# A four-layer recurrent network on one core: the first layer's tail is folded into its experts, and the last layer's attention gets another order on TensorE

## The chip, the core and the metric

The kernel runs as one program on one core of a Trainium2 chip. The metric is the device time of one execution in microseconds (us); less is better. The engines that compute are TensorE (PE in the profile; its weight loads stand apart as PEld), VectorE (DVE), ScalarE (ACT) and GpSimd (POOL); SyncE (SP) issues the transfers. Semaphores are all that orders the engines between each other.

## What is computed

The input is x of 8 sequences by 512 tokens by 128 features. Each of four layers normalises x, runs an attention `s` and a feed-forward part `f` on the same normalised xn, and adds their gated product:

```
xn = layernorm(x)
s = attention_l(xn, ...)
g = silu(ffn_l(xn, ...))
x = x + s * g
```

Two pieces matter here.

The first layer's attention (differential, 16 heads of 8) ends in a normalisation of each head's output and a projection; its feed-forward part has two shared experts of weight 1/2 and four routed ones, of which a token takes the two with the largest softmax weight:

```
normed = (heads - mu) * rsqrt(var + EPS) * ln_w + ln_b
attention = normed.reshape(b, s, H * DH) @ wo
weights = softmax(x @ gate_w + gate_b);  topk_w, topk_i = top_k(weights, 2)
shared = (relu(x @ sw1 + sb1) @ sw2 + sb2).sum(axis=2) / 2
routed = (gather(relu(x @ rw1 + rb1) @ rw2 + rb2, topk_i) * topk_w).sum(axis=2)
```

The last layer's attention is causal, with 16 heads of 64 and a relative bias:

```
logits = (einsum('bhqd,bhkd->bhqk', q, k) + causal + bias) / dh
out = einsum('bhqk,bhkd->bhqd', softmax(logits), v)
return out.reshape(B, T, H * dh) @ Wo + bo
```

## The kernel before, in words

A sequence's 512 tokens are four blocks of 128 (`QT = 4`). Each layer is a row of phases; a phase is a block of its own with its own tiles and semaphores, and no engine begins the next one until all have ended the last. `R.xnT` holds xn with the features on the partitions, `R.s` and `R.f` the two results. Within a phase each engine has a program written out by hand; `run_bodies` writes the first and the last trip apart and loops over those between. There is no scheduler: the order on an engine is the order of its code.

**First layer's tail.** After `attend_phase` has left the heads' outputs in `heads`, five phases follow. `outproj_phase` (L889, "out") goes through the 8 sequences: DVE centres (`center`, L917 and L919), ACT squares (L970), DVE sums (L925), ACT takes the root (L976), DVE inverts and scales (L929, L933), PE transposes four blocks (`turn`, L1020), ACT moves them out of PSUM (`leave`, L983), PE multiplies by `wo` (`project`, L1028), and ACT copies the result to `R.s` (L989). `logits_phase` (L1052, "lg") computes the gate, four values a token, with the gate's weights as the loaded operand and xn as the moving one, and turns them back (L1072, L1079). `top2_phase` (L1103, "top") takes the softmax and the two largest on DVE. `turn_weights_phase` (L1190, "turn") transposes the weights and multiplies them by the output biases, which gives the first content of `R.f` (L1255, L1263, L1224). `experts_phase` (L1269, "ex") runs the six experts in three trips of two. A trip has 16 groups `g` (two experts by eight sequences); a group has four steps `u`: `up` (L1331, 128x512) into one of two PSUM banks `ph`, ReLU on ACT (L1366), `down` (L1340, four of 128x128) into `po`; one `up` goes ahead of each `down`. DVE adds the weighted `po` into `R.f` once a group (L1382).

**Last layer's attention** (`layer3_attention`, L1872, "att"). For each of 8 sequences it runs 8 pairs of heads, 64 pairs `m` in all, and each pair has four steps `j`, one for each block of queries; `s` counts the steps of a sequence. Because of the causal mask step j is (j+1)*128 keys wide. For a pair PE does: three projections into the one bank `pA` (k=0 gives qT, k=1 kT, both L1985; k=2 gives v, L1988), each moved out by ACT (`leave`, L2089); for each step the `scores` (L2000), whose two heads take the upper and the lower 64 rows of the array, three steps ahead (`AHEAD`); `turn` of the two heads' softmax rows (L2010); `weigh` (L2027), whose two heads take 64 columns of the array each, into `pO`; and once a pair `through_wo` (L2036), which also goes to `pA`. ACT moves `pO` out (`outputs`, L2111). DVE adds the bias and finds the row's extreme (`extreme`, L2160), inverts the row sums (`invert`, L2166), adds `pA` to `R.s` (`add`, L2180) and copies the turned rows to `WT` (L2174; for step 1 it is ACT, L2105). ACT takes the exponentials (`expo`, L2097), POOL divides (L1958). `WT` is a ring of four rows, two a step. The order around a step is

```
if j % 2 == 1: scores(s + 3); scores(s + 4)
if j == 0: project(1, m + 1)
if j == 1: through_wo(m - 1)
if j == 2: project(2, m + 1)
if j == 3: project(0, m + 2)
turn(2 * s + 2); turn(2 * s + 3)
weigh(s)
```

## Time and profile before

| | |
|---|---|
| median of 3 runs | 3879.37 us (3876.12 to 3881.76) |
| the profiled execution's own time | 3873.31 us |
| its span | 3871.5 us |
| mean granted TensorE clock | 0.914 of 2.4 GHz |
| busy PE, DVE, ACT, POOL | 87%, 61%, 52%, 40% of the span |
| first layer's tail, from the last write to `heads` to the last write to `R.f` | 678.2 to 1104.7 us |
| last layer's attention, steady part | 3017 to 3786 us |

The profiled execution is one run with every instruction's start and duration in it. Its time is 1.8 us above its span and 6.1 us under the median. A share of busy time is a mean over stages that have different limits, so the stages are read apart.

### The profile page before, as it was taken

How to read it: one execution, taken by the hardware profiler on the slowest of the kernel's cores; microseconds unless marked ns; L12 is line 12 of the kernel's file. 1: busy time of each engine (PE TensorE's matmuls, PEld its weight loads, DVE VectorE, ACT ScalarE, POOL GpSimd, SP SyncE). 2: the span in 40 equal slices, each digit the busy share in tenths (PEclk: the TensorE clock that was granted, in tenths of full speed). 3: DMA queues.
4: the chain of work that ended last, by engine and by line, in shares of the span. 5: the costliest groups of instructions: out<-in, count | busy, mean ns of one | idle time of the engine just before them, and what ended most of it. 6: DMA issues, size and time to landing. Idle time of an engine off the chain costs nothing. (4 is left out here: it accounts for less than half of the span.)

```text
span 3871.5 us, 87522 instructions
## 1 busy us (share of the span) xinstructions
PE 3381.1 (87%) x26932; PEld 2090.2 (54%) x26932; DVE 2358.0 (61%) x5961; ACT 2030.5 (52%) x4194; POOL 1567.7 (40%) x2652
## 2 busy tenths in 40 slices
PE   5799999599966999959999947979874999999997
PEld 2344444477742222226777723579863666666664
DVE  5688887311135888856777765258356566666664
ACT  5588888333353788833333353333253566666552
POOL 0367676000010232316777717045472444444440
PEclk9799999799986999979999968877696999999999
DMA  5422222000013111116666411300023333333330
GB/s 138 102 73 74 73 73 54 12 6 12 6 36 89 45 44 46 41 27 173 163 156 161 117 58 37 102 12 3 9 50 55 127 115 114 118 115 113 114 101 22
DMA packets 199845, 289.31 MB, mean 75 GB/s; under 512 B 40954, under 2 KB 156864, under 8 KB 199252
## 3 DMA queue, kind: packets, MB, share of 16 engines
q1 hardware_dynamic: 195480, 277.41, 25.8%
q0 software_dynamic: 4096, 8.40, 1.5%
q8 instruction: 158, 2.59, 0.3%
q14 instruction: 111, 0.91, 0.1%
HBM read 234.41 MB, written 35.93 MB: 70 GB/s over the span
## 5 line engine op out<-in xcount | busy, mean ns | idle before, releaser
L779 ACT ACTIVATE att_E<-att_pX,att_gs 128x512 f32<-128x512 f32 x1152 | 718.7, 684 | 128.3 <-PE att_pX L708 127.6
L1958 POOL TENSOR_TENSOR att_E<-att_E,att_rz 128x128 f32<-128x128 f32 (+3 forms) x512 | 358.2, 721 | 433.6 <-DVE att_rz L2166 433.6
L834 DVE TENSOR_REDUCE att_mx<-att_pS 128x2 f32<-128x1024 f32 (+2 forms) x448 | 434.6, 991 | 82.2 <-PE att_pS L686 68.3
L686 PE MATMUL att_pS<-arr_ks,arr_qs 72*128 72x512 bf16 (+4 forms) x1536 | 421.4, 338 | 51.8 <-DVE att_mx L834 28.4
L708 PE MATMUL att_pX<-arr_qs,arr_ks 75*128 75x512 bf16 (+4 forms) x1536 | 419.2, 328 | 8.5 <-DMA arr_qs<-att_mp 4.4
L1698 POOL TENSOR_TENSOR pairs_h<-pairs_m,pairs_r 128x512 f32<-128x512 f32 x272 | 346.1, 1273 | 190.9 <-DVE pairs_m L1761 181.7
L1722 PEld LDWEIGHTS pairs_po<-pairs_a,pairs_h 128*128 128x128 f32 x2176 | 286.3, 192 | 130.3 <-issue 128.5
L826 DVE CUSTOM_DVE_ANT_0 att_seen<-att_pS,arr_later 128x384 bf16<-128x384 f32 (+1 forms) x512 | 298.8, 613 | 80.3 <-PE att_pS L686 79.9
L1743 ACT ACTIVATE pairs_r<-pairs_ph 128x512 f32<-128x512 f32 x272 | 162.6, 598 | 327.1 <-PE pairs_ph L1714 327.1
L721 PE MATMUL att_pO<-att_E,att_vs 128*9 128x512 f32 (+3 forms) x3072 | 296.8, 488 | 8.8 <-ACT att_E L779 8.4
L2097 ACT ACTIVATE att_E<-att_S,att_nm 128x128 f32<-128x128 f32 (+3 forms) x512 | 282.1, 556 | 39.6 <-DVE att_nm L2160 39.4
L1714 PE MATMUL pairs_ph<-xnT,pairs_a 128*128 128x512 f32 x544 | 281.4, 600 | 10.2 <-DMA pairs_a<-in_down_dram 10.2
L1722 PE MATMUL pairs_po<-pairs_a,pairs_h 128*128 128x128 f32 x2176 | 287.5, 275 | 0.3 <-POOL pairs_h L1698 0.3
L617 POOL TENSOR_SCALAR_AFFINE_SELECT att_E<-att_E 128x256 f32<-128x256 f32 (+1 forms) x640 | 228.5, 361 | 136.4 <-ACT att_E L779 131.1
L686 PEld LDWEIGHTS att_pS<-arr_ks,arr_qs 76*128 76x128 bf16 (+1 forms) x1536 | 133.9, 98 | 258.9 <-DVE att_mx L834 100.0
L1761 DVE SCALAR_TENSOR_TENSOR pairs_m<-pairs_ph,pairs_c 128x512 f32<-128x512 f32 x272 | 187.9, 692 | 140.4 <-ACT pairs_r L1743 132.2
L2160 DVE CUSTOM_DVE_ANT_0 att_S<-att_pS,att_bias 128x128 f32<-128x128 f32 (+3 forms) x512 | 230.5, 487 | 67.4 <-PE att_pS L2000 62.0
L708 PEld LDWEIGHTS att_pX<-arr_qs,arr_ks 127*128 127x128 bf16 (+1 forms) x1536 | 149.0, 98 | 217.0 <-ACT att_E L779 124.4
L1340 PEld LDWEIGHTS ex_po<-ex_a,ex_h 128*128 128x128 f32 x1536 | 201.6, 192 | 91.8 <-issue 91.0
L1366 ACT ACTIVATE ex_h<-ex_ph,ex_bs 128x512 f32<-128x512 f32 x192 | 132.0, 687 | 213.5 <-PE ex_ph L1331 213.5
L1382 DVE SCALAR_TENSOR_TENSOR f<-ex_po,ex_ws,f 128x128 f32<-128x128 f32 x192 | 54.1, 344 | 276.7 <-PE ex_po L1340 276.7
L2174 DVE COPY att_WT<-att_pT 128x128 f32<-128x128 f32 (+2 forms) x384 | 178.8, 507 | 66.2 <-PE att_pT L2010 59.0
(410 smaller groups left out, 6531.1 us busy)
## 6 DMA issues: line engine op xcount, KB each, us to landing
pairs_c<-weights SPq DMA_DIRECT2D x272, 256.0 KB, 4.0
att_bias<-in_bias_dram SPq DMA_DIRECT2D x64, 896.0 KB, 4.6
parts<-proj_part SPq DMA_DIRECT2D x144, 128.0 KB, 2.3
att_xb<-xnT SPq DMA_DIRECT2D x64, 256.0 KB, 2.7
arr_qs<-parts SPq DMA_DIRECT2D x192, 64.0 KB
arr_ks<-parts SPq DMA_DIRECT2D x192, 64.0 KB
att_w<-in_w3a_dram SPq DMA_DIRECT2D x64, 192.0 KB, 2.4
arr_qs<-parts SPq DMA_DIRECT2D x96, 96.0 KB
```

Source lines behind the costliest of these rows:

```text
L686: ins = nc.tensor.matmul(pS[:, bank, n * w:(n + 1) * w], qs[:K1, u, x, q * P:(q + 1) * P], ks[:K1, u, x, :w], start=(n == 0 or not causal) ...
L708: ins = nc.tensor.matmul(pX[:, bank, o:o + w], ks[:, g % NB, x, kt * P:(kt + 1) * P], qs[:, g % NB, x, q0(kt):], start=(n == 0), stop=True ...
L721: ins = nc.tensor.matmul(pO[32 * x:32 * x + DV, q0(kt):], vs[:, g % 2, x // maps, kt], E[:, cell_of[x, kt] % NE, o:o + w], start=(kt == OR ...
L779: nc.scalar.activation(E[:, c % NE], pX[:, BANK2[(g * NP2 + c) % (NB * NP2)]], ACT.Exp, scale=gs[:, g % 2, gain_of:gain_of + 1]).then_inc( ...
L826: V.tensor_tensor_reduce(out=seen[:, own, :w], in0=pS[:, bank, :w], in1=arr.later[:, T - w:], scale=1.0, scalar=-3.0e38, op0=ALU.add, op1= ...
L834: V.reduce_max(dst, src, AX.X).then_inc(s_mx, 1)
L1698: nc.gpsimd.tensor_tensor(h[:, g % RING], m[:, g % RING], r[:, g % RING], ALU.mult).then_inc(s_h, 1)
L1714: nc.tensor.matmul(ph[:, g % RING], a[:, v, 0], R.xnT[:, b * T:(b + 1) * T], start=True, stop=True).then_inc(s_up, 1)
L1722: ins = nc.tensor.matmul(po[:, g % RING, q * P:(q + 1) * P], h[:, g % RING, q * P:(q + 1) * P], a[:, v, 1], start=True, stop=True)
L1958: nc.gpsimd.tensor_tensor(E[:, k, :width(j)], E[:, k, :width(j)], rz[:, u, k:k + 1].broadcast_to([P, width(j)]), ALU.mult).then_inc(s_n, 1)
L2097: nc.scalar.activation(E[:, k, :width(j)], S[:, r % RING, :width(j)], ACT.Exp, bias=nm[:, u, k:k + 1], scale=-1.0, accum_out=Z[:, u, k:k + ...
L2160: nc.vector.tensor_tensor_reduce(out=S[:, r % RING, :w_], in0=pS[:, r // 2 % 2, h, :w_], in1=bias[:, u, off:off + w_], scale=-1.0 / DW, sc ...
```

## The change

In the first layer, `first_tail_phase` takes the place of all five phases. The experts' order is turned: the shared two come first (first trip), the routed four after them. Before the experts PE computes the gate by 32 small matmuls, with xn as the loaded operand and the four gate columns as the moving one; into the first trip's 16 groups are put the normalisation and projection of the 8 sequences, a piece after a step of a group, and the softmax and choice of the two largest. Their functions `center`, `variance`, `scale`, `square`, `root`, `leave`, `result` are those of `outproj_phase`; `top_two` and `shifted` are `top2_phase`'s. The output biases are now added by DVE, four 128x128 instructions a group in the second and third trip; the shared experts' bias `c2` comes in with the first write of `R.f`. `ph` and `h` have four buffers in place of two, and two `up`s go ahead.

In the last layer, `weigh` of two steps stands together at every even step, two steps late, with the next two `scores` right behind; all three projections of a pair move by a place, and `WT` has eight rows. `through_wo` now waits for the pair's v to have left `pA`.

```diff
-        outproj_phase(nc, R, "out0", heads, out)
+        first_tail_phase(nc, R, "ex0", heads, out, gate, t["lower4"], t["w1_0"], t["b1_0"], t["w2_0"], t["b2_0"])
...
+def first_tail_phase(nc, R, name, heads, out, gate, lower, w1, b1, w2, b2):
...
+    NE, NR, U, HB = 6, 4, 4, 4
...
+        ph = p.ps("ph", [P, HB, T])
         po = p.ps("po", [P, 2, T])
-        s_b = p.sem("b")
+        pT = p.ps("pT", [P, T])
+        pY = p.ps("pY", [P, QT, D])
...
+        pl = pY[:, :, :].rearrange("p q d -> p (q d)")[:, :NT * NR]
...
                 sp.dma_start(bb[:, :, :], b1).then_inc(s_b, 16)
+                sp.dma_start(lo[:, :], lower).then_inc(s_lo, 16)
...
+                    if first:
+                        sp.dma_start(b2r[:, :, :], b2).then_inc(s_b2, 16)
...
+                pe.wait_ge(s_g, 32)
+                for n in range(NT):
+                    ins = nc.tensor.matmul(pl[:, n * NR:(n + 1) * NR], R.xnT[:, n * P:(n + 1) * P], gw, start=True, stop=True)
+                ins.then_inc(s_lg, 1)
+                pe.wait_ge(s_o, loads)
+
+                def turn(n):
+                    pe.wait_ge(s_hb, n + 1)
+                    if n >= 1:
+                        pe.wait_ge(s_hT, n)
+                    for q in range(QT):
+                        ins = nc.tensor.transpose(pT[:, q * P:(q + 1) * P], hb[:, n % 4, q], R.ident[:, :])
+                    ins.then_inc(s_t, 1)
+
+                def project(n):
+                    if n == 0:
+                        pe.wait_ge(s_sub, 1)
+                    pe.wait_ge(s_hT, n + 1)
+                    if n >= 1:
+                        pe.wait_ge(s_out, n)
+                    for q in range(QT):
+                        ins = nc.tensor.matmul(pY[:, q], hT[:, n % 2, q * P:(q + 1) * P], wo, start=True, stop=True)
+                    ins.then_inc(s_y, 1)
...
-                        if not (first and k < 2):
-                            pe.wait_ge(s_h, at(IT * U, k - 1))
-                        nc.tensor.matmul(ph[:, u % 2], a1[:, v, u], R.xnT[:, b * T:(b + 1) * T], start=True, stop=True).then_inc(s_up, 1)
+                        if not (first and k < HB):
+                            pe.wait_ge(s_h, at(IT * U, k - HB + 1))
+                        nc.tensor.matmul(ph[:, u], a1[:, v, u], R.xnT[:, b * T:(b + 1) * T], start=True, stop=True).then_inc(s_up, 1)
...
                     if first:
                         up(0)
+                        up(1)
                     for k in range(IT * U):
-                        if not (last and k + 1 >= IT * U):
-                            up(k + 1)
-                        down(*divmod(k, U))
+                        g, u = divmod(k, U)
+                        if not (last and k + 2 >= IT * U):
+                            up(k + 2)
+                        down(g, u)
+                        if first and u == 1 and 0 <= g - 4 < B:
+                            turn(g - 4)
+                        if first and u == 3 and 0 <= g - 5 < B:
+                            project(g - 5)
...
+                            if not first:
+                                continue
+                            if g == 0 and u == 3:
+                                act.wait_ge(s_sub, 1)
+                                nc.scalar.activation(pr[:, :, :], pr[:, :, :], ACT.Exp).then_inc(s_exp, 1)
+                            if u == 0 and 0 <= g - 1 < B:
+                                square(g - 1)
+                            if u == 1 and 0 <= g - 6 < B:
+                                result(g - 6)
+                            if u == 2 and 0 <= g - 4 < B:
+                                leave(g - 4)
+                            if u == 3 and 0 <= g - 2 < B:
+                                root(g - 2)
...
+                        if first:
+                            if g == 0:
+                                V.memset(eps[:, :], EPS).then_inc(s_eps, 1)
+                                shifted()
+                                shared_bias()
+                            if g == 1:
+                                top_two()
+                            if g < B:
+                                center(g)
+                            if 0 <= g - 2 < B:
+                                variance(g - 2)
+                            if 0 <= g - 3 < B:
+                                scale(g - 3)
+                            dve.drain()
+                            dve.wait_ge(s_d, at(IT, g + 1))
+                            for q in range(QT):
+                                ins = V.scalar_tensor_tensor(out=tiles[q], in0=po[:, g % 2, q * P:(q + 1) * P], scalar=0.5,
+                                                             in1=tiles[q] if v else c2[:, :], op0=ALU.mult, op1=ALU.add)
+                            ins.then_inc(s_f, 1)
+                            continue
...
+                        V.tensor_copy(ws[:, g % 2], wts[:, b * QT:(b + 1) * QT, bass.ds(i * 2 + (v - 2), 1)])
                         dve.drain()
...
+                            V.scalar_tensor_tensor(out=tiles[q], in0=b2r[:, bass.ds(i * 2 + v, 1), :].rearrange("p o d -> p (o d)"), scalar=ws[:, g % 2, q],
+                                                   in1=tiles[q], op0=ALU.mult, op1=ALU.add)
+                        dve.drain()
+                        dve.wait_ge(s_d, at(IT, g + 1))
+                        for q in range(QT):
+                            ins = V.scalar_tensor_tensor(out=tiles[q], in0=po[:, g % 2, q * P:(q + 1) * P], scalar=ws[:, g % 2, q],
+                                                         in1=tiles[q], op0=ALU.mult, op1=ALU.add)
...
-    RING = 4
+    RING, WR = 4, 8
...
-                    if k == 2 and not (first and m < 2):
-
-                        pe.wait_ge(s_add, at(PAIRS, m - 1))
+                    if k == 0 and not (first and m < 3):
+                        pe.wait_ge(s_add, at(PAIRS, m - 2))
                     elif not (first and m == 0 and k == 0):
                         pe.wait_ge(s_pc, at(3 * PAIRS, 3 * m + k))
...
                 def through_wo(at, m, ahead):
                     pe.wait_ge(s_oc, at(PAIRS, m + 1))
                     if ahead:
-                        pe.wait_ge(s_pc, at(3 * PAIRS, 3 * (m + 2) + 2))
+                        pe.wait_ge(s_pc, at(3 * PAIRS, 3 * (m + 2) + 3))
+                    else:
+                        pe.wait_ge(s_add, at(PAIRS, m))
...
-                        project(at, 0, 1, True)
-                        for t_ in range(AHEAD + 1):
+                        for k in range(2):
+                            project(at, k, 1, True)
+                        for t_ in range(AHEAD):
                             scores(at, t_, True)
                         turn(at, 0, True)
                         turn(at, 1, True)
                     for s in range(STEPS):
                         m, j = divmod(s, QT)
-                        if j % 2 == 1 and not (last and s + AHEAD >= STEPS):
-                            scores(at, s + AHEAD, first)
-                            scores(at, s + AHEAD + 1, first)
+                        if j % 2 == 0:
+                            for t_ in (s - 2, s - 1):
+                                if not (first and t_ < 0):
+                                    weigh(at, t_, first)
+                            for t_ in (s + AHEAD, s + AHEAD + 1):
+                                if not (last and t_ >= STEPS):
+                                    scores(at, t_, first)
                         if j == 0 and not (last and m + 1 >= PAIRS):
-                            project(at, 1, m + 1, first)
+                            project(at, 2, m + 1, first)
                         if j == 1 and not (first and m == 0):
                             through_wo(at, m - 1, not (last and m + 1 >= PAIRS))
-                        if j == 2 and not (last and m + 1 >= PAIRS):
-                            project(at, 2, m + 1, first)
-                        if j == 3 and not (last and m + 2 >= PAIRS):
-                            project(at, 0, m + 2, first)
+                        if j >= 2 and not (last and m + 2 >= PAIRS):
+                            project(at, j - 2, m + 2, first)
                         if not (last and s + 1 >= STEPS):
                             turn(at, 2 * s + 2, first)
                             turn(at, 2 * s + 3, first)
-                        weigh(at, s, first)
                     if last:
-
-                        pe.wait_ge(s_add, at(PAIRS, PAIRS - 1))
+                        weigh(at, STEPS - 2, False)
+                        weigh(at, STEPS - 1, False)
...
-                    if not (first and r < RING):
-                        act.wait_ge(s_o, at(STEPS, r // 2 - 1))
-                    nc.scalar.activation(WT[:, r % RING, :width(j)], pT[:, r % 2, :width(j)], ACT.Copy).then_inc(s_wa, 1)
+                    if not (first and r < WR):
+                        act.wait_ge(s_o, at(STEPS, r // 2 - 3))
+                    nc.scalar.activation(WT[:, r % WR, :width(j)], pT[:, r % 2, :width(j)], ACT.Copy).then_inc(s_wa, 1)
...
-                        leave(at, 0, 1, True)
+                        for k in range(2):
+                            leave(at, k, 1, True)
...
-                            leave(at, 1, m + 1, first)
-                        if j == 2 and not (last and m + 1 >= PAIRS):
                             leave(at, 2, m + 1, first)
-                        if j == 3 and not (last and m + 2 >= PAIRS):
-                            leave(at, 0, m + 2, first)
+                        if j >= 2 and not (last and m + 2 >= PAIRS):
+                            leave(at, j - 2, m + 2, first)
...
+    t["w1_0"], t["b1_0"], t["w2_0"] = experts(*(np.concatenate([inp[f"L0_ffn_s{k}"], inp[f"L0_ffn_r{k}"]]) for k in ("w1", "b1", "w2")))
+    t["b2_0"] = rows(np.concatenate([inp["L0_ffn_sb2"], inp["L0_ffn_rb2"]])[None], 6, D)
```

Where it moves instructions, three places.

PE, first layer's tail, before (out, lg, turn and ex are the phases; a row counts instructions of one kind on end, "4x512" is the result's shape):

```order
L1020 MATMUL out_pT<-ident,out_hb 128x128 x4
L1028 MATMUL out_pY<-pre_wo,out_hT 128x128 x8
...
L1072 MATMUL lg_pl<-xnT,pre_gw 4x512 x2
L1079 MATMUL lg_pt<-ident,lg_lT 128x4 x8
...
L1255 MATMUL turn_pt<-ident,turn_st 6x128 x8
L1263 MATMUL turn_pf<-turn_b,turn_wt 128x128 x8
...
L1331 MATMUL ex_ph<-xnT,ex_a 128x512 x2
L1340 MATMUL ex_po<-ex_a,ex_h 128x128 x4
L1331 MATMUL ex_ph<-xnT,ex_a 128x512
```

and with the change, at the phase's start and in the groups 4 and 5 of its first trip:

```order
L1184 MATMUL ex_pY<-pre_gw,xnT 128x4 x32
L1216 MATMUL ex_ph<-xnT,ex_a 128x512 x3
L1225 MATMUL ex_po<-ex_a,ex_h 128x128 x4
L1216 MATMUL ex_ph<-xnT,ex_a 128x512
...
L1225 MATMUL ex_po<-ex_a,ex_h 128x128 x4
L1193 MATMUL ex_pT<-ident,ex_hb 128x128 x4
L1216 MATMUL ex_ph<-xnT,ex_a 128x512
...
L1225 MATMUL ex_po<-ex_a,ex_h 128x128 x4
L1203 MATMUL ex_pY<-pre_wo,ex_hT 128x128 x4
L1216 MATMUL ex_ph<-xnT,ex_a 128x512
```

The transposes and the products of the `out` phase, which stood ahead, now stand after the second and the fourth step of a group; those of `lg` and `turn` are gone but for the 32 small ones.

PE, last layer's attention, before, from the turning of step 0 on, twelve rows of a pair of heads (pS scores, pT turned rows, pO weighed, pA with w a projection, with wo the output product):

```order
L2010 MATMUL att_pT<-ident,att_E 128x128 x2
L2027 MATMUL att_pO<-att_WT,att_v 64x128 x8
L1985 MATMUL att_pA<-att_xb,att_w 128x512
L2010 MATMUL att_pT<-ident,att_E 128x128 x4
L2027 MATMUL att_pO<-att_WT,att_v 64x128 x2
L2000 MATMUL att_pS<-att_kT,att_qT 128x128 x2
L2000 MATMUL att_pS<-att_kT,att_qT 128x256 x2
L2036 MATMUL att_pA<-pre_wo,att_oT 128x128 x4
L2010 MATMUL att_pT<-ident,att_E 128x128 x6
L2027 MATMUL att_pO<-att_WT,att_v 64x128 x4
L1988 MATMUL att_pA<-att_w,att_xb 128x128 x4
L2010 MATMUL att_pT<-ident,att_E 128x128 x8
```

and with the change, from the weighing of a pair's steps 2 and 3 on:

```order
L2025 MATMUL att_pO<-att_WT,att_v 64x128 x14
L1998 MATMUL att_pS<-att_kT,att_qT 128x512 x2
L1998 MATMUL att_pS<-att_kT,att_qT 128x128 x2
L1986 MATMUL att_pA<-att_w,att_xb 128x128 x4
L2008 MATMUL att_pT<-ident,att_E 128x128 x4
L2036 MATMUL att_pA<-pre_wo,att_oT 128x128 x4
L2008 MATMUL att_pT<-ident,att_E 128x128 x6
L2025 MATMUL att_pO<-att_WT,att_v 64x128 x6
L1998 MATMUL att_pS<-att_kT,att_qT 128x256 x2
L1998 MATMUL att_pS<-att_kT,att_qT 128x384 x2
L1983 MATMUL att_pA<-att_xb,att_w 128x512
L2008 MATMUL att_pT<-ident,att_E 128x128 x8
```

Four places of weighing have become two, v's projection stands two short pieces ahead of the output product, and the scores of steps 3 and 0 now stand together, as do those of 1 and 2.

ACT, the same pair, before:

```order
L2089 ACTIVATE att_qT<-att_pA 128x512
L2097 ACTIVATE att_E,att_Z<-att_S,att_nm 128x384 x2
L2111 ACTIVATE att_oT<-att_pO 128x512
L2089 ACTIVATE att_kT<-att_pA 128x512
L2105 ACTIVATE att_WT<-att_pT 128x256 x2
L2097 ACTIVATE att_E,att_Z<-att_S,att_nm 128x512 x2
L2097 ACTIVATE att_E,att_Z<-att_S,att_nm 128x128 x2
L2089 ACTIVATE att_v<-att_pA 128x512
L2097 ACTIVATE att_E,att_Z<-att_S,att_nm 128x256 x2
```

and with the change:

```order
L2113 ACTIVATE att_oT<-att_pO 128x512
L2091 ACTIVATE att_v<-att_pA 128x512
L2107 ACTIVATE att_WT<-att_pT 128x256 x2
L2099 ACTIVATE att_E,att_Z<-att_S,att_nm 128x512 x2
L2099 ACTIVATE att_E,att_Z<-att_S,att_nm 128x128 x2
L2091 ACTIVATE att_qT<-att_pA 128x512
L2099 ACTIVATE att_E,att_Z<-att_S,att_nm 128x256 x2
L2091 ACTIVATE att_kT<-att_pA 128x512
L2099 ACTIVATE att_E,att_Z<-att_S,att_nm 128x384 x2
```

`leave` of v now stands ahead of the copies to `WT` and of the exponentials of step 3 (128x512), where that of kT stood.

## Rows read from the trace of the kernel before

**Rows 1.** Busy time by stage, first layer's tail (stretch; length; PE, PEld, DVE, ACT, POOL; PE clock; DMA)
```profile
670.00:710.00 40.00, 20.75 (x160) 14.78 (x148) 26.25 (x49) 23.60 (x42) 3.54 (x10) 0.83 0.00 1
...
767.00:870.00 103.00, 103.00 (x583) 74.46 (x582) 18.15 (x70) 40.55 (x59) 0.19 (x1) 0.99 0.02 6
```
**Rows 2.** Timeline, first layer's tail (start, us, engine, line, op, idle before)
```profile
676.70 0.66 PE L729 MATMUL att_pS<-ident,att_oT 128*128 128x128 f32 x4 [0.72 <-ACT att_oT L791]
...
695.95 0.65 PE L1020 MATMUL out_pT<-ident,out_hb 128*128 128x128 f32 x4 [1.41 <-DVE out_hb L933]
696.44 1.06 PE L1028 MATMUL out_pY<-pre_wo,out_hT 128*128 128x128 f32 x8
...
765.30 3.49 PE L1331 MATMUL ex_ph<-xnT,ex_a 128*128 128x512 f32 x4 [5.33 <-DMA ex_a<-in_w_dram]
...
679.83 0.06 DVE L947 MEMSET out_eps<- 128x1 f32 x1 [1.60 <-PEq L50]
```
**Rows 3.** Busy time by shorter stretches, same columns
```profile
681.00:683.00 2.00, 0.00 (x0) 0.00 (x0) 1.92 (x4) 0.94 (x2) 0.00 (x0) 0.50 0.00 0
...
724.00:732.00 8.00, 0.00 (x0) 0.00 (x0) 5.81 (x18) 1.59 (x2) 0.00 (x0) 0.71 0.01 1
...
736.00:761.00 25.00, 20.79 (x90) 16.51 (x88) 6.13 (x14) 4.24 (x8) 0.00 (x0) 0.50 0.00 1
```
**Rows 4.** Timeline of PE, second layer's projections at 1.2 GHz
```profile
1162.14 1.86 PE L394 MATMUL proj_pm<-proj_kblk,proj_qf 128*128 128x16 f32 x8 [1.29 <-DVE proj_kblk L455]
1163.84 3.76 PE L378 MATMUL proj_ps<-xnT,pre_w 128*128 128x512 f32 x4
```
**Rows 5.** Busy time by stage, last layer's attention, same columns
```profile
3200.00:3300.00 100.00, 99.26 (x799) 67.69 (x796) 61.27 (x224) 60.16 (x184) 46.73 (x66) 1.00 0.37 121
```
**Rows 6.** Timeline of PE, one pair of heads in the last layer's attention
```profile
3200.24 1.16 PE L2036 MATMUL att_pA<-pre_wo,att_oT 128*128 128x128 f32 x8
...
3201.24 0.82 PE L2010 MATMUL att_pT<-ident,att_E 128*128 128x128 f32 x6
...
3201.98 0.66 PE L2027 MATMUL att_pO<-att_WT,att_v 128*64 128x128 f32 x8
...
3202.72 1.16 PE L1988 MATMUL att_pA<-att_w,att_xb 128*128 128x128 f32 x8
...
3205.49 1.77 PE L2000 MATMUL att_pS<-att_kT,att_qT 64*128 64x384 f32 x8
...
3208.47 1.09 PE L2027 MATMUL att_pO<-att_WT,att_v 128*64 128x128 f32 x16
...
3209.49 1.13 PE L1985 MATMUL att_pA<-att_xb,att_w 128*128 128x512 f32 x2
...
3210.46 0.60 PE L2010 MATMUL att_pT<-ident,att_E 128*128 128x128 f32 x4
...
3210.99 0.44 PE L2027 MATMUL att_pO<-att_WT,att_v 128*64 128x128 f32 x4
...
3211.36 1.04 PE L2000 MATMUL att_pS<-att_kT,att_qT 64*128 64x128 f32 x8
...
3212.32 1.16 PE L2036 MATMUL att_pA<-pre_wo,att_oT 128*128 128x128 f32 x8
```
**Rows 7.** Waits of PE's weight load of L1988, whole run (releaser: us, times)
```profile
  DVE s L2180: 25.8, 70
```
**Rows 8.** Timeline of ACT and DVE, the same pair
```profile
3210.66 0.60 ACT L2089 ACTIVATE att_kT<-att_pA 128x512 f32<-128x512 f32 x1
...
3211.68 0.73 ACT L2097 ACTIVATE att_E<-att_S,att_nm 128x512 f32<-128x512 f32 x1
...
3213.23 0.17 DVE L2166 RECIPROCAL att_rz<-att_Z 128x2 f32<-128x2 f32 x1 [1.60 <-ACT att_E L2097]
...
3213.89 0.08 DVE L2160 DVE_READ_ACCUMULATOR2_ANT att_nm<- 128x1 f32 x1
```
**Rows 9.** Timeline of PE, start of the last layer's attention at 1.2 GHz
```profile
3009.32 2.05 PE L1985 MATMUL att_pA<-att_xb,att_w 128*128 128x512 f32 x2 [0.78 <-ACT att_v L2089]
```

302 lines of the change are left out of this document (116 added, 186 removed).

## The prediction

> **What bounds the kernel now.** I read the busy times by stage first, to see which engine is full where the change works. In the experts PE is busy 103.00 of 103 us while ACT is busy 40.55 and DVE 18.15 [rows 1]; the first of them waits 5.33 us for its weights and starts at 765.30, though the last work of the attention on PE starts at 676.70 [rows 2]. Between lie phases in which PE is half idle: from 670 to 710 it is busy 20.75 of 40 us [rows 1], and from 724 to 732 not at all [rows 3]. So the tail is a chain of phases, and what leaves it is worth its whole length. The last layer's attention is different: PE is busy 99.26 of 100 us at a granted clock of 1.00, and no other engine over 61.27 [rows 5]. There only PE's own time counts. I take it from the timeline, where a pair of heads repeats after 3212.32 - 3200.24 = 12.08 us [rows 6].
>
> About 0.2% (7.8 us) is what a measurement of this kernel can tell from no change.
>
> **First layer, the start.** The new phase begins where the old one did, DVE's first instruction at 679.83 [rows 2]; I give PE 680.1. Its first work is the gate: 32 products with 128 loaded columns and 4 moving ones, each of two instructions. No row has that shape. The nearest has 16 moving columns: 8 instructions take 1163.84 - 1162.14 = 1.70 us, 0.2125 each, at 1.2 GHz [rows 4]. At 2.4 GHz half of that is the bound from below. PE's clock was already down at 681 to 683, at 0.50 of full speed [rows 3], after an idle time like the one that remains, so the gate starts at 1.2 GHz. I take 64 x 0.2125 = 13.6 us (bounds 6.8 and 13.6), to 693.7. The experts' weights were waited for at most 5.33 us [rows 2]; here they go behind two small transfers, at about 680, so they land under the gate. The biases `b2r` stand behind them on SP's queue and are needed only at the end of group 0. The first `up` then starts at 693.7 in place of 765.30: **71.6 us gained**. All of `out`, `lg`, `top`, `half`, `turn` and their borders are in that number. The experts' own slow start, 3.49 us for the first four instructions [rows 2], is there in both.
>
> **First layer, what PE gets back.** Eight sequences cost a `turn` of four, 696.44 - 695.95 = 0.49 us [rows 2], and a `project`, taken at 3201.24 - 3200.24 = 1.00 from a product of the same shape [rows 6]: 8 x 1.49 = **11.9 us lost**. The experts' own steps stay as they are: PE was full, so a second `up` ahead buys nothing there, and is only cover.
>
> **First layer, what lies beside.** ACT was busy 23.60 us in the 40 us that hold all eight sequences [rows 1], so at most 2.95 a sequence; a group of 7.0 us holds 0.39 x 7.0 = 2.8 of ReLU. Together 5.7 of the 8.5 us of a group that carries work: hidden by PE. DVE: 26.25 / 8 = 3.3 and 1.2 of its own [rows 1], 4.5 us: hidden. Group 1 also holds the choice of two, 5.81 us [rows 3], so DVE has 10.3 us of work in 7.0. Two `po` banks cover the late add; but `square(1)` waits on ACT for the late `center(1)` with ReLUs queued behind it. By my walk DVE ends `center(1)` 1.5 us into group 2, the ReLU of its step 1 ends at 2.8 and PE wants it at 2.6: 0.3 us lost with a wake-up (bounds 0 and 10.3 - 7.0 = 3.3). In the 32 groups of the later trips DVE adds four 128x128 instructions, by its own add of the same shape 1.2 us, into 5.8 idle ones: nothing; without that idle time it would be 38 us. Sum: 71.6 - 11.9 - 0.3 = **59.4 us gained**.
>
> **Last layer, PE.** A weighing of n instructions takes 0.37 us to the next piece for n = 4 and 1.02 for n = 16 [rows 6]: 0.054 each and 0.15 on leaving. A turn takes 0.53 for 4 and 0.74 for 6: 0.105 each and 0.11 on going to the weighing. Merging four weighings into two saves 2 x (0.15 + 0.11) = 0.52 us a pair. The weighing of eight before v's projection takes 0.74 where the rule gives 0.58: 0.16 is PE waiting for DVE's add [rows 6], one of 70 such waits [rows 7]; with the new order the add has 3 us, and this goes too. Two turns now stand before products: 0.49 - 4 x 0.105 = 0.07 each [rows 2], 0.14 back. Gross gain 0.54 us.
>
> **Last layer, the new wait.** v's projection and the output product share `pA`, and between them stands only a turn of four. A projection that starts at 3209.49 is copied out by ACT from 3210.66 to 3211.26 [rows 8], and the scores waiting for that copy start at 3211.36 [rows 6]: start plus 1.87. PE reaches the output product at start plus 1.00 + 0.49 = 1.49. It waits 0.38 us in every pair; behind it stand the next turns. Before, that projection was followed by 2.7 us of other work, so the trace has no such wait; 0 and 0.5 are my ends. Net 0.54 - 0.38 = 0.16 us, times 64: **10.2 us gained**. The start of the phase has one projection more ahead of the first scores, 2.05 + 0.78 at 1.2 GHz [rows 9], and 1.0 less later: **1.8 lost**.
>
> **Sum.** 59.4 + 10.2 - 1.8 = 67.8 us. The profiled execution's 3873.3 becomes 3805.5. Its time lies 6.1 us under the median, so the median of 3879.4 becomes 3811.6, rounded 3812.
>
> **Rivals.**
>
> *The gate is faster.* If the gate gets 2.4 GHz as early as the experts did, whose first four instructions took 3.49 us [rows 2], the first 14 or so of 64 instructions are slow (3.0 us) and 50 take half (5.3): 8.3 us, and the median 3807. Against it: from 736 to 761 PE was busy 20.79 of 25 us with small products, and the clock stayed at 0.50 [rows 3]. The Trainium skill (TensorE: Matmul & The Clock Gate, What's actually happening) calls the warm-up a budget of time, whatever is issued; that rule sides with this rival, and the row last named does not agree with it. Chance 0.17.
>
> *No wait in the last layer.* If ACT frees `pA` in time, 0.54 x 64 = 34.6 us: 3787. The projection's copy starts 1.17 us after it begins whatever I do, so 0.08.
>
> *The last layer gains nothing.* On ACT the copy of v, then the copies to `WT`, now stand ahead of step 3's exponentials. Walk, from the pair's first weighing: v's projection at 0.15 + 28 x 0.054 + half of the scores' 2.8 (1.77 + 1.04 [rows 6]) = 3.1; exponentials at 3.1 + 1.17 + 1.02 (3210.66 to 3211.68 [rows 8]) = 5.3; DVE's inversion 1.55 later, 6.8 (3211.68 to 3213.23); the extremes of the next step 0 behind it 0.74 later, 7.6. PE wants those for the scores of step 2: output product at 4.9, turn 5.9, weighings 6.7, scores of step 1 7.5, of step 2 at 8.0. The slack is 0.4 us. If other waits eat it and 0.16 more, the last layer is even: 3879.4 - 59.4 + 1.8 = 3822; half a microsecond beyond, 3854. POOL's division for step 3 has 0.7 us. Chance 0.14.
>
> *The first trip is bound by ACT or DVE*, because pieces wait for each other in order: at most ACT's 2.95 us in each of eight groups, 24 us: 3835. Against it 2.8 us of room in a group. This is also the case in which the tail is not really hidden. Chance 0.07.
>
> *Slower.* The chain of the third rival, far longer: if the extremes come late by over 0.4 + (67.8 + 7.8) / 64 = 1.6 us, every pair pays more than everything gained. At 2.4 us late a pair costs 2.0 more, 128 us: 3940. DVE is idle 39 of 100 us and ACT 40 [rows 5], which speaks against it. Chance 0.03.
>
> **Numbers.** Forecast 0.50, the rivals 0.17, 0.08, 0.14, 0.07 and 0.03, no change 0.01. The forecast's own spread is the gate (6.8 us), the wait (0 to 0.5 a pair, so -8 to +24) and group 1 (3 us). The range 3792 to 3836 holds it nearly all, the first rival, the fourth and the better half of the third; the wait-free case (0.08), the worse half of the third (0.07) and the slower one (0.03) lie outside, 0.18. Faster 0.96, the same 0.01, slower 0.03.
>
> **What would show it.** In the new profile: 64 instructions of L1184 over 13 to 14 us with the clock at 0.50; the first `up` at 693 to 695; PE without idle time to the tail's end at 1045; ACT and DVE under 70% in the first trip; the last layer repeating after 11.9 us, with a wait of L2036 on ACT's `att_v` of 0.4 to 0.7 us a pair, gap included, and none of L1986 or L1983 on DVE's add. The forecast is wrong if the gate takes under 9 us, if a pair takes under 11.6 or over 12.1 us, or if PE idles between groups 1 and 12.

## The result and the profile after

| | before | changed |
|---|---|---|
| median (4 runs each, one chip) | 3879.3 us | 3820.3 us (3816.0 to 3826.9) |
| ratio | | 0.985 (0.9831 to 0.9869) |
| profiled execution, its span | 3873.3, 3871.5 us | 3826.9, 3825.1 us |
| mean granted clock | 0.914 | 0.916 |
| first layer: experts' first `up` | 765.30 | 695.48 |
| last layer's attention, first projection to the next stage's first product | 790.1 us | 791.7 us |

The change saves 59.0 us (50.8 to 65.6 by the interval) where 67.8 were forecast. The predicted 3812 lies 8 us under the measured time, inside the range; the whole gain, and somewhat more, is in the first layer. Its profile shows the tail as it was drawn. The timeline of PE there:

```profile
678.74 0.66 PE L729 MATMUL att_pS<-ident,att_oT 128*128 128x128 f32 x4 [0.72 <-ACT att_oT L791]
681.83 13.78 PE L1184 MATMUL ex_pY<-pre_gw,xnT 128*128 128x4 f32 x64 [2.44 <-PEq L50]
695.48 4.20 PE L1216 MATMUL ex_ph<-xnT,ex_a 128*128 128x512 f32 x6
...
1041.53 2.84 PE L1225 MATMUL ex_po<-ex_a,ex_h 128*128 128x128 f32 x24
1056.48 1.11 PE L182 MATMUL norm_pT<-ident,norm_xn 128*128 128x128 f32 x4 [12.12 <-ACT norm_xn L140]
```

In this execution the attention ended 2.04 us later than in the one before (678.74 against 676.70 [rows 2]). On the clock of before, the first `up` therefore starts at 693.4. Busy times by stage (stretch; length; PE, PEld, DVE, ACT, POOL; PE clock; DMA), the gate first, then the first `up`s behind it:

```profile
682.00:695.00 13.00, 13.00 (x62) 13.00 (x63) 0.00 (x0) 0.00 (x0) 0.32 (x2) 0.50 0.35 114
695.00:698.00 3.00, 3.00 (x6) 1.63 (x7) 2.03 (x7) 0.34 (x1) 0.00 (x0) 0.50 0.00 0
698.00:700.00 2.00, 2.00 (x9) 1.10 (x8) 0.55 (x1) 1.32 (x3) 0.00 (x0) 0.93 0.00 0
...
720.00:760.00 40.00, 40.00 (x244) 30.20 (x243) 21.15 (x50) 21.69 (x39) 0.19 (x1) 1.00 0.01 2
800.00:900.00 100.00, 100.00 (x574) 72.75 (x573) 30.22 (x115) 39.23 (x58) 0.37 (x2) 1.00 0.04 11
```

The gate runs at the lower clock from end to end; behind it PE is full, with DVE and ACT at just over half of the 40 us that hold most of the sequences' work. PE, half empty in [rows 1] and at rest in [rows 3], has no idle time left here.

In the last layer PE is busy 96.59 of 100 us where it was 99.26 [rows 5]:

```profile
3200.00:3300.00 100.00, 96.59 (x810) 68.86 (x811) 59.59 (x226) 61.84 (x182) 47.16 (x68) 1.00 0.36 112
```

and one pair of heads takes 3163.69 - 3151.63 = 12.06 us, against 12.08 [rows 6]:

```profile
3151.63 1.75 PE L2025 MATMUL att_pO<-att_WT,att_v 128*64 128x128 f32 x28
3153.31 1.35 PE L1998 MATMUL att_pS<-att_kT,att_qT 64*128 64x512 f32 x8
3154.59 1.16 PE L1986 MATMUL att_pA<-att_w,att_xb 128*128 128x128 f32 x8
3155.59 0.60 PE L2008 MATMUL att_pT<-ident,att_E 128*128 128x128 f32 x4
3156.53 1.13 PE L2036 MATMUL att_pA<-pre_wo,att_oT 128*128 128x128 f32 x8 [0.34 <-ACT att_v L2091]
3157.49 0.82 PE L2008 MATMUL att_pT<-ident,att_E 128*128 128x128 f32 x6
3158.24 0.88 PE L2025 MATMUL att_pO<-att_WT,att_v 128*64 128x128 f32 x12
3159.05 1.35 PE L1998 MATMUL att_pS<-att_kT,att_qT 64*128 64x256 f32 x8
3160.33 1.12 PE L1983 MATMUL att_pA<-att_xb,att_w 128*128 128x512 f32 x2
3161.29 1.04 PE L2008 MATMUL att_pT<-ident,att_E 128*128 128x128 f32 x8
3162.16 1.10 PE L1983 MATMUL att_pA<-att_xb,att_w 128*128 128x512 f32 x2
3163.10 0.66 PE L2008 MATMUL att_pT<-ident,att_E 128*128 128x128 f32 x2
3163.69 1.75 PE L2025 MATMUL att_pO<-att_WT,att_v 128*64 128x128 f32 x28
```

Read start to start, that is from the start of one row to the start of the next. The turn at 3155.59 holds PE 0.94 us; a turn of four before a product without a wait takes 0.49 [rows 2]. So PE waits 0.45 us, of which the view shows 0.34 as idle. The turn of two at 3163.10 holds it 0.59. Its second transpose goes into the `pT` bank that row 7 (the second head's step 3) is still being copied out of, by DVE (`pT` has two banks, and a row of a pair goes into bank row modulo 2):

```profile
3162.02 1.29 DVE L2175 COPY att_WT<-att_pT 128x512 f32<-128x512 f32 x2 [0.47 <-PE att_pT L2008]
```

The copy of rows 6 and 7 ends at 3163.31. This second wait has no row in the view of PE's waits, since it falls between two transposes that the timeline shows as one. From 3000 to 3650 us that list has only

```profile
PE att_pA L2036 <- ACT att_v L2091: 18.5, 54, 0.3
```

Two questions follow: is the whole gain the first layer's, and are these two waits what ate the last layer's?

### The profile page after: what moved, and what is told of

Read it like the earlier page. It is cut to its first block and busy times, and to the rows that moved or that the text cites. A ratio compares the mean times of both kernels' runs of the same rounds, so it can differ in the third digit from the quotient of the medians.

```text
span 3825.1 us, 87256 instructions
## 1 busy us (share of the span) xinstructions
PE 3345.6 (87%) x26852; PEld 2091.7 (55%) x26852; DVE 2373.0 (62%) x6059; ACT 2026.3 (53%) x4169; POOL 1563.8 (41%) x2652
## 5 line engine op out<-in xcount | busy, mean ns | idle before, releaser
L598 POOL CAST att_mp<-att_m 16x128 bf16<-16x128 f32 x288 | 80.5, 280 | 311.8 <-ACT att_m L785 286.6
L2008 PE MATMUL att_pT<-ident,att_E 128*128 128x128 f32 x1280 | 194.3, 274 | 10.1 <-DVE att_WT L2175 2.1
```

## The experiments

The runs were made on four chips, on which the kernel before took 3879.3, 3854.3, 3853.7 and 3873.8 us. So every row is compared by its ratio to the kernel before on its own chip; "a pair" is the time after which the pairs of heads repeat in the steady part (us), and "phase" is the last layer's attention in the profile (us), as above. Two kernels are compared by their medians only where they ran on one chip, or else by their ratios and phases.

| kernel | this, us | before, us | ratio (95%) | a pair | phase |
|---|---|---|---|---|---|
| changed kernel, first chip | 3820.3 | 3879.3 | 0.9850 (0.9831 to 0.9869) | 12.06 | 791.7 |
| tail alone | 3794.3 | 3854.3 | 0.9842 (0.9829 to 0.9856) | 12.09 | 789.0 |
| attention alone | 3859.9 | 3854.3 | 1.0013 (1.0004 to 1.0022) | 12.06 | 791.8 |
| output product later | 3807.1 | 3854.3 | 0.9874 (0.9858 to 0.9889) | 12.28 | 806.3 |
| row 7 on ACT | 3776.9 | 3854.3 | 0.9796 (0.9782 to 0.9809) | 11.78 | 773.9 |
| changed kernel again | 3796.8 | 3853.7 | 0.9857 (0.9842 to 0.9872) | 12.06 | 791.6 |
| later, copies exchanged | 3786.9 | 3853.7 | 0.9824 (0.9810 to 0.9837) | 11.88 | 780.7 |
| v between the scores | 3766.2 | 3853.7 | 0.9771 (0.9758 to 0.9784) | 11.56 | 761.4 |
| gate in group 0 | 3800.0 | 3853.7 | 0.9861 (0.9846 to 0.9876) | 12.06 | 791.6 |
| v between, again | 3784.7 | 3873.8 | 0.9774 (0.9761 to 0.9787) | 11.56 | 761.4 |
| another start | 3781.7 | 3873.8 | 0.9761 (0.9748 to 0.9774) | 11.56 | 757.1 |
| step 0 turned later | 3793.3 | 3873.8 | 0.9793 (0.9780 to 0.9807) | 11.74 | 772.7 |

**The two halves.** The tail alone is the changed kernel with the last layer's attention of before; the attention alone is the reverse. Of the first, the lines that decide the order on PE:

```diff
-                        if j % 2 == 0:
-                            for t_ in (s - 2, s - 1):
-                                if not (first and t_ < 0):
-                                    weigh(at, t_, first)
...
+                        if j % 2 == 1 and not (last and s + AHEAD >= STEPS):
+                            scores(at, s + AHEAD, first)
+                            scores(at, s + AHEAD + 1, first)
...
+                        weigh(at, s, first)
```

> The changed kernel with the last layer's attention of the kernel before: only the first layer's tail is moved into the experts. Theory A (the first layer is worth what its own steps show: first up at 693 to 695, eight turns and projections at about 1.3 to 1.5 us each, and nothing else lost): 57 to 62 us less than before, 3817 to 3822 by the shown median of 3879.4, and norm1's first transposes about 60 us earlier. Theory B (the unchanged first-layer code behind norm1 really takes some 10 us more once it runs 60 us earlier, as the profile of the changed kernel shows by landmarks: 60.1 us ahead at norm1, 50.2 at norm2): 47 to 52 us less, and the last layer of the changed kernel was then worth about 10 us. The profile decides too: under A the lead at norm2 equals that at norm1 within 2 us, under B it is 8 to 12 us smaller.

> The kernel before with only the last layer's attention changed. If the forecast's term holds (net 0.16 us a pair, start 1.8 us dearer): 8.4 us less than before, 0.998. Rival, by the profile of the changed kernel (a pair takes 12.06 where it took 12.08, because output product and first row of the next turn wait 0.45 and 0.27 us where 0.74 was saved; its attention took 791.6 us against 790.1): between 0 and 2 us more than before, ratio 0.999 to 1.001. In its profile both would show the wait of L2036-like output product on ACT's copy of v near 0.3 us a pair.

The tail alone gains 60.0 us and the attention alone loses 5.6 (1.5 to 8.5). Of the 5.6 the phase itself shows 2.8 (791.8 - 789.0); the rest is inside the interval and was not traced. From norm1's first transposes to the last layer's first projection the one takes 1863.2 us and the other 1862.7, on one chip: unchanged code does not pay for starting earlier. The nearly 12 us that the two first profiles differ by in that stretch (1884.4 and 1896.2) are a difference between executions: three kernels that are alike there took 1878.8, 1880.0 and 1890.1 on another chip. Theory B of the first expectation falls.

**The changed kernel again**, beside others.

> The changed kernel itself, beside the experiments on one chip. From the two halves measured alone (60.0 us less with the tail only, 5.6 us more with the last layer's attention only) 54 us less than before is expected, a ratio of 0.986; the forecast's own sum would be 67.8 us, 0.9825. Its stretch from norm1's first transposes to the last layer's first projection should be within 1.5 us of before's on the same chip, if the first layer's unchanged code loses nothing (1863.2 with the tail changed, 1862.7 with it not, on one chip).

56.9 us less (49.3 to 60.9). That is 2.5 from the sum of the halves, 54.4, which is inside the interval here and in the first result's (50.8 to 65.6); the forecast's 67.8 is outside both. From norm1's first transposes to the last layer's first projection it takes 1862.1 us. No trace of the kernel before was kept on this chip, so this compares only with the two halves.

**The output product behind the next turns.** It reaches the bank of v later, so the first wait should go.

```diff
-                        if j == 1 and not (first and m == 0):
-                            through_wo(at, m - 1, not (last and m + 1 >= PAIRS))
...
                             turn(at, 2 * s + 3, first)
+                        if j == 1 and not (first and m == 0):
+                            through_wo(at, m - 1, not (last and m + 1 >= PAIRS))
```

> The changed kernel with the output product issued behind the next turns (of six) in place of ahead of them: it then reaches the bank of v's projection at start plus about 2.6 us, when ACT's copy (start plus 1.87 in the trace before) has long freed it. Theory A (the wait on v's bank costs its 0.45 us in full): a pair 11.6 us, 64 x 0.45 = 28 us less than the changed kernel. Theory B (the chain of ACT's copies, exponentials, DVE's inversion and extremes has almost no slack and sets the pair once that wait is gone): the wait turns up at the scores of step 2 or at row 7's turn, and the gain is under 10 us. Between them if the second wait (0.27 us, row 7) grows with it.

A miss: it gains 47.2 us on before where the changed kernel gains 56.9, and a pair is 0.22 us longer, the phase 14.7. PE and ACT in its timeline:

```profile
3160.92 0.60 PE L2008 MATMUL att_pT<-ident,att_E 128*128 128x128 f32 x4
3161.12 0.60 ACT L2091 ACTIVATE att_v<-att_pA 128x512 f32<-128x512 f32 x1 [1.76 <-PE att_pA L1986]
3161.61 0.65 ACT L2107 ACTIVATE att_WT<-att_pT 128x256 f32<-128x256 f32 x2
3162.13 0.85 PE L2008 MATMUL att_pT<-ident,att_E 128*128 128x128 f32 x6 [0.62 <-ACT att_WT L2107]
```

The wait on v is gone, but the next turns need the `pT` banks that ACT empties behind the copy of v. From turn to turn PE now spends 1.21 us in place of 0.49, a wait of 0.72 for one of 0.45. The old wait had been covering this one. That is neither of the two places that theory B named.

**The same with the copies exchanged:** rows 2 and 3 by DVE, row 7 by ACT.

```diff
-    BY_ACT = (2, 3)
+    BY_ACT = (7,)
```

> The changed kernel with the output product behind the next turns, the copies of rows 2 and 3 given to DVE (idle there for 2.4 us, while ACT has copy of v, two copies and exponentials in a row) and row 7's copy to ACT. Theory A (moving the output product alone lost because the next turns then waited 0.62 us for ACT's copies of rows 2 and 3, which stand behind the copy of v): both waits go, and row 7's too: a pair 11.3 to 11.45 us, 64 x 0.65 = 42 us less than the changed kernel. Theory B (PE's pieces simply cost more in this order): a pair stays at 11.9 or above.

A pair takes 11.88: row 7's wait is gone, and the one at the next turns is 1.09 - 0.49 = 0.60 (3162.35 to 3163.44 in its timeline), now on DVE, which takes the copies up behind its extremes, at 3162.87. Only a part of theory A came true: 0.18 us a pair and 10.0 us in all, where some 0.65 and 42 were expected. Which engine copies was not the point; with either, a turn of four is too little work between two users of `pT`.

**Row 7's copy on ACT**, all else as changed.

```diff
-    BY_ACT = (2, 3)
+    BY_ACT = (2, 3, 7)
```

> The changed kernel with the copy of turned row 7 out of PSUM given to ACT in place of DVE. Theory A (the first turn of step 0 waits 0.27 us in each pair for DVE's copy of row 7, which stands behind other DVE work; ACT has idle time there): that wait goes, 64 x 0.27 = 17 us less than the changed kernel. Theory B (ACT's 0.5 us more in a pair come ahead of its next exponentials and the late extremes are what PE waits for): no gain, or up to 20 us more. If the attribution in the profile to POOL's work is right and not the copy, the same time within 4 us and the wait stays in its place.

```profile
3163.77 0.38 PE L2008 MATMUL att_pT<-ident,att_E 128*128 128x128 f32 x2
3164.08 1.75 PE L2025 MATMUL att_pO<-att_WT,att_v 128*64 128x128 f32 x28
```

The turn of two falls from 0.59 to 0.31 and the pair from 12.06 to 11.78, all of it that wait. It gains 77.4 us on before, some 20 more than the changed kernel on other chips (59.0 and 56.9), where 17 were expected; the phase is 17.7 us shorter. It also settles what PE waited for. In the changed kernel the list of waits of PE's weight loads puts L2008 down to POOL's division 51 times from 3020 to 3640 us, 0.2 us each; here that row stays, 53 times, and the wait is gone. So it was the copy and not the division.

**Step 0 turned later:** the same wait taken away by order, with every copy left on its engine.

```diff
+                        if j == 0 and not (first and s == 0):
+                            turn(at, 2 * s, first)
+                            turn(at, 2 * s + 1, first)
...
-                        if not (last and s + 1 >= STEPS):
+                        if j < 3:
                             turn(at, 2 * s + 2, first)
                             turn(at, 2 * s + 3, first)
```

> The changed kernel with the turns of each pair's step 0 issued behind the weighings and scores instead of ahead of them; all copies stay on their engines. Row 7's copy on DVE then has 3 us until the pT bank is wanted again. If that copy was the second wait: it goes here too (a pair 11.8, 17 us less than the changed kernel). Rival: DVE's copies of the step-0 rows come later and the turns of step 1 behind v's projection, or the output product, wait for them: a pair at 12.0 or above.

11.74 a pair, and the phase 18.9 us shorter than the changed kernel's: theory A, a little better than expected. Two ways to the same end agree.

**v's projection between the two scores,** with row 7 on ACT. This shrinks the other wait without moving the output product behind anything.

```diff
-                            for t_ in (s + AHEAD, s + AHEAD + 1):
-                                if not (last and t_ >= STEPS):
-                                    scores(at, t_, first)
-                        if j == 0 and not (last and m + 1 >= PAIRS):
-                            project(at, 2, m + 1, first)
+                            if not (last and s + AHEAD >= STEPS):
+                                scores(at, s + AHEAD, first)
+                            if j == 0 and not (last and m + 1 >= PAIRS):
+                                project(at, 2, m + 1, first)
+                            if not (last and s + AHEAD + 1 >= STEPS):
+                                scores(at, s + AHEAD + 1, first)
```

> The changed kernel with row 7's copy on ACT, and v's projection issued between the two scores in place of behind them, so that 0.28 us more of other work lies between it and the output product. If the output product waits for the bank until start plus 1.94, it reaches it at start plus 1.77 and waits 0.17 in place of 0.45: a pair 11.50 us (11.78 without this edit), 18 us less than with row 7's copy on ACT alone. Rival: the scores of the next pair's step 0, issued 1.0 us later, come late for DVE's extremes (slack 0.4 us by the forecast's walk): a pair at or above 11.78. By the trace DVE takes them up 5 us after they are issued, which speaks for the first.

```profile
3162.87 1.16 PE L1986 MATMUL att_pA<-att_w,att_xb 128*128 128x128 f32 x8
3163.96 0.49 PE L1998 MATMUL att_pS<-att_kT,att_qT 64*128 64x128 f32 x4
3164.38 0.66 PE L2008 MATMUL att_pT<-ident,att_E 128*128 128x128 f32 x4
3164.87 1.06 PE L2036 MATMUL att_pA<-pre_wo,att_oT 128*128 128x128 f32 x8
```

PE's list of waits has no row of the output product any more. It starts 2.00 us after v's projection does; the two pieces ahead of it got longer, 1.09 for 1.00 and 0.42 for the 0.28 that I had counted. In the changed kernel the product started 1.94 us after the projection, as soon as the bank was free (3154.59 to 3156.53), so here it arrives just behind that. A pair takes 11.56 where 11.50 was expected: the wait shrank by all its 0.45, and the pieces cost 0.23 more. The phase is 12.5 us shorter than with row 7 alone, where 18 were expected. The run on another chip confirmed it:

> The same kernel as the one with v's projection between the scores and row 7's copy on ACT, beside the next two on one chip: 0.977 of before again (87 us less), a pair 11.56 us, 761.4 us from the attention's first projection to the next stage.

**Another start.** The second pair's k is projected behind the first three scores; on ACT its copy follows four exponentials.

```diff
-                        for k in range(2):
-                            project(at, k, 1, True)
+                        project(at, 0, 1, True)
                         for t_ in range(AHEAD):
                             scores(at, t_, True)
+                        project(at, 1, 1, True)
...
-                        for k in range(2):
-                            leave(at, k, 1, True)
-                        for r in range(2 * AHEAD):
+                        leave(at, 0, 1, True)
+                        for r in range(4):
+                            expo(at, r, True)
+                        leave(at, 1, 1, True)
+                        for r in range(4, 2 * AHEAD):
                             expo(at, r, True)
```

> That kernel with another start of the last layer's attention: the second pair's k is projected behind the first three scores instead of ahead of them, and ACT copies it out behind four exponentials. Theory A (the start lost 5.6 us where 1.8 were forecast, because a projection and its copy, 2.74 us at the lower clock, stand ahead of the first scores and everything behind waits for them): the first turn starts 2.7 us earlier, at start plus 14.9 in place of 17.6, and the phase is 2 to 4 us shorter than the kernel it is made from (757 to 759 us). Theory B (the start is bound by ACT's and POOL's chain of exponentials and divisions, and the projection only moves its place): less than 1 us shorter.

```profile
2945.67 2.05 PE L1983 MATMUL att_pA<-att_xb,att_w 128*128 128x512 f32 x2 [4.98 <-DMA att_xb<-xnT]
...
2955.99 2.82 PE L1998 MATMUL att_pS<-att_kT,att_qT 64*128 64x128 f32 x12
2958.74 1.12 PE L1983 MATMUL att_pA<-att_xb,att_w 128*128 128x512 f32 x2
2960.66 0.68 PE L2008 MATMUL att_pT<-ident,att_E 128*128 128x128 f32 x2 [0.79 <-POOL att_E L1957]
```

The first turn comes at start plus 14.99 (17.6 without the edit), the phase is 4.3 us shorter (757.1 against 761.4), and the medians differ by 3.0 us. The intervals overlap, so the whole time does not tell the two apart; the phase shows theory A, and a second gain that it did not name. The 2.6 us at the first turn are not all: the next two pieces, scores and v's projection, take 2.15 us here (2961.27 to 2963.42) and 3.76 without the edit (2954.81 to 2958.57). In the run without it PE had rested 1.84 us before the first turn, and the granted clock is 0.66 from 2955 to 2960; here PE rested 0.79 us, and it is 1.00 from 2958.7 to 2962. 2.6 and 1.6 are the 4.3.

**The gate inside group 0,** behind its second step, when PE is at work.

```diff
                         down(g, u)
+                        if first and k == 1:
+                            logits()
```

> The changed kernel with the gate's 32 products issued inside group 0 (behind its second step) in place of ahead of it: PE waits for the experts' weights first, and the gate runs when PE has been working for some us. Theory A (its 13.78 us were the clock's lower level, nothing else): 64 instructions in 6.9 us at granted clock 1.00, first up at 685 to 686 in place of 695.5, and 3 us less in all, since 3.5 us of waiting for weights come back. Theory B (products with 4 moving columns cost 0.21 us each whatever the clock): 13.7 us inside group 0, and 3 to 4 us more in all.

3.2 us slower by the medians, not 3 faster; the intervals overlap, so the stages have to say it. Its timeline of PE and its busy times:

```profile
686.21 5.46 PE L1218 MATMUL ex_ph<-xnT,ex_a 128*128 128x512 f32 x6 [6.97 <-DMA ex_a<-in_w_dram]
...
694.44 9.53 PE L1187 MATMUL ex_pY<-pre_gw,xnT 128*128 128x4 f32 x64
703.82 2.06 PE L1218 MATMUL ex_ph<-xnT,ex_a 128*128 128x512 f32 x2
```

```profile
694.00:697.00 3.00, 3.00 (x30) 3.00 (x28) 0.00 (x0) 0.44 (x1) 0.00 (x0) 1.00 0.02 5
697.00:700.00 3.00, 3.00 (x25) 3.00 (x24) 0.00 (x0) 0.00 (x0) 0.00 (x0) 0.83 0.00 0
700.00:704.00 4.00, 4.00 (x20) 4.00 (x21) 0.00 (x0) 0.00 (x0) 0.00 (x0) 0.50 0.00 0
```

Both theories miss the gate: it takes 9.4 us where 6.9 or 13.7 were expected. It starts at the upper clock, and while it runs, PE without a gap, the clock falls to the lower one. It stays there for the next two steps, which take 6.22 us (703.82 to 710.04) in place of 3.52. With this the loss adds up. Against the changed kernel on the same chip, from the attention's end on: first `up` 9.0 us earlier, gate 9.4 back, the first steps 1.1 slower, the two behind the gate 2.7; sum 4.2. Norm1 comes 4.2 us later, again from the attention's end. That is the loss that theory B named, for another reason.

## Why the prediction was right or wrong

**First layer, the start: right.** 13.78 us for the 64 instructions at clock 0.50, against 13.6; first `up` at 693.4 on the clock of before, against 693.7. The rival of the faster gate is out, and the gate in group 0 shows more than that: even where it began at a granted clock of 1.00, the clock was 0.50 before it ended. The row that the forecast set against the rival, 736 to 761, holds other shapes (6 loaded columns or 6 rows, each with 128 moving columns); it pointed the right way, but it was not the gate's case.

**First layer, what PE gets back: right, slightly too dear.** From the first `up` to the last `down` 1044.37 - 695.48 = 348.9 us, against 338.2 before: 10.7 lost, where turns, projections and group 1 were to cost 12.2. The idle time at the border is 12.12 us, 0.9 less than before. A turn takes 0.44 us here and a projection 0.90, where 0.49 and 1.00 were counted. ACT and DVE stayed hidden as forecast; the `down` of group 2's step 1, the one that the forecast named, comes 0.2 us late, where 0.3 was expected. The term was 59.4, and the tail alone measured 60.0 (55.5 to 65.9).

**Last layer, PE: the gross gain was too small.** 0.54 us a pair was forecast. Taking both waits from the new pair leaves 12.06 - 0.45 - 0.28 = 11.33, so 0.75 was gained. 0.12 of the difference is in the scores, which I had costed at nothing: four steps take 1.28 + 1.28 us now, and 1.71 + 0.97 in the old order (start to the next piece's start, in the timeline of the tail alone). The remaining 0.09 is spread over the other pieces in the same two timelines: without the waits the four products into `pA` take 3.86 us for 3.93, and the four turns 2.42 for 2.55 where a saving of 0.08 was counted. The weighings went as the rule said, 2.49 us for 2.93.

**Last layer, the new wait: right in place, low in size, and not alone.** 0.45 us for 0.38 on v's bank. The step that failed is net 0.54 - 0.38 = 0.16: it followed the bank `pA` through the new order, and not the two banks of `pT`. In the new order the turns of step 3 stand one projection (0.94 us) ahead of the next pair's step 0, and the copies of two full rows take DVE 1.29 us from 3162.02. That costs 0.28 us, 18 us in 64 pairs. Two experiments show it by removing it in different ways (11.78 and 11.74). Waits of 0.73 ate a gain of 0.75.

**Last layer, the start: mis-sized.** 1.8 us forecast; the first output product comes 5.6 us later after the first projection than with the old order. In the tail alone, and in the changed kernel run again on another chip:

```profile
2920.30 2.04 PE L1984 MATMUL att_pA<-att_xb,att_w 128*128 128x512 f32 x2 [5.01 <-DMA att_xb<-xnT]
...
2934.93 0.69 PE L2009 MATMUL att_pT<-ident,att_E 128*128 128x128 f32 x2 [0.71 <-POOL att_E L1957]
...
2949.66 1.16 PE L2035 MATMUL att_pA<-pre_wo,att_oT 128*128 128x128 f32 x8
```

```profile
2917.53 2.04 PE L1983 MATMUL att_pA<-att_xb,att_w 128*128 128x512 f32 x2 [4.99 <-DMA att_xb<-xnT]
...
2935.55 0.69 PE L2008 MATMUL att_pT<-ident,att_E 128*128 128x128 f32 x2 [1.85 <-POOL att_E L1957]
...
2937.95 2.07 PE L1986 MATMUL att_pA<-att_w,att_xb 128*128 128x128 f32 x8
...
2952.50 1.13 PE L2036 MATMUL att_pA<-pre_wo,att_oT 128*128 128x128 f32 x8 [0.34 <-ACT att_v L2091]
```

29.36 and 34.97 us. The first turn is 3.4 us later (14.63, 18.02), because PE waits on POOL for 1.1 us more on top of the projection. I took back 1.0 us for work saved later, but the scores and v's projection behind the first turn run slowly again, at a granted clock of 0.61 from 2936 to 2940: the projection at 2937.95 takes 1.86 us to its next piece where the old order's takes 0.99. That PE's longer rest let the clock fall fits the other start, where it rests less and the clock stays. Between the first output product and the last but one 3.4 us are gained (748.8 to 745.4), and 0.5 lost behind. About half of the 3.4 is the gain in every pair, under 0.03 us; the rest is mostly that seven pairs of the old order take 12.28 to 12.45 us and none of the new over 12.15. Sum: 2.7 us longer, where 8.4 shorter was forecast.

**Rivals.** "The last layer gains nothing" came true in its size but not by its mechanism: PE's list of waits in the steady part has none for extremes or exponentials. The slower case and the ACT-bound first trip did not come. The 8 us between forecast and result lie in the last layer: measured apart, the first layer came within 1 us of its term (60.0 for 59.4), and the last layer on the wrong side of zero (its phase 2.7 us longer, where 8.4 us less was forecast).

**Luck.** That the forecast missed by no more is in part luck. In 64 pairs the second wait, which it did not see, cost 18 us, and the first 4 more than counted; the pieces of the new order saved 13 more than counted. These errors have nothing to do with each other, and they left the pair at 12.06 us, 0.14 over the forecast, and not at 12.27.

**The best version.** The changed kernel with row 7 on ACT, v between the scores and the other start takes 0.9761 of before (0.9748 to 0.9774), 92 us less on its chip, and beats both kernels; against the same kernel without the other start the whole time shows no difference, only the phase does. Its phase is 34.5 us shorter than the changed kernel's: 30.2 by the two waits, net of the dearer pieces (791.6 - 761.4), and 4.3 by the start.

## What to carry to other kernels

When an order is rewritten, walk every bank that has one writer and one reader, not only the one that the edit names: for each, start of the write, work in between, end of the copy out. A wait can cover another; taking one away by moving a piece may just hand it to the next, so look for a place where independent work can be put between, and let the engine's own timeline say how much is enough. Moving the work of idle phases into a full one paid all it promised here (60.0 us for 59.4), and could be costed from rows alone.

## What was not expected of the hardware

Being busy alone did not keep PE's granted clock up here, nor bring it up. In the run with the gate in group 0 its products (128 loaded columns, 4 moving) began at 2.4 GHz and, with PE busy all the time, the granted clock went from 1.00 to 0.83 and then 0.50 in the three stretches shown above. In the changed kernel they kept PE busy 13.00 of 13.00 us at 0.50, and the clock rose only behind the first `up`s, with 512 moving columns: 0.50 from 695 to 698, 0.93 from 698 to 700. The Trainium skill (TensorE: Matmul & The Clock Gate, What's actually happening) calls the warm-up a budget of time, not of instructions, with everything behind it at the upper level. With the wide products of this kernel the trace agrees; with the gate's neither run does. By that rule the gate in group 0 would have taken some 6.9 us, an estimate from half of the 13.78 measured at the lower level.
